# Five of 26 score masks of a cross attention are added by VectorE instead of TensorE

## The reference

```python
scores = jnp.einsum('bhqd,bhkd->bhqk', qh, kh) / jnp.sqrt(jnp.float32(D_K))
scores = jnp.where(mask == 0, NEG_INF, scores)
attn = jax.nn.softmax(scores, axis=-1)
ctx = jnp.einsum('bhqk,bhkd->bhqd', attn, vh)
```

## Time and profile before

| | us |
|---|---|
| median of 3 runs | 3214.25 (3211.05 to 3221.2) |
| profiled execution | 3217.97, its span 3216.2 |
| PE busy | 2959.7 (92%) |
| DVE busy | 2314.7 (72%) |
| ACT busy | 1707.0 (53%) |
| POOL busy | 455.9 (14%) |
| masked cross attention, first to last mask product | 696.1 to 1407.0 |

### The profile page before, as it was taken

One profiled execution on the slowest core, in us unless ns is written; L12 is line 12 of the kernel. 1 busy time (PEld: TensorE's weight loads), 2 busy tenths in 40 slices (PEclk: granted clock), 3 DMA queues, 4 the chain that ended last, 5 costly groups with the idle time before them and its releaser, 6 DMA issues. The chain is left out here.

```text
span 3216.2 us, 96994 instructions
## 1 busy us (share of the span) xinstructions
PE 2959.7 (92%) x41243; PEld 1694.4 (53%) x41243; DVE 2314.7 (72%) x5743; ACT 1707.0 (53%) x2152; POOL 455.9 (14%) x553
## 2 busy tenths in 40 slices
PE   5999999999999999982999999989999999989994
PEld 2666666546655565541466665553333333366662
DVE  6788888587777777748788886238999999551114
ACT  2366667525555555550477776312777777722220
POOL 0255562020000000000222212001100000001113
PEclk8899999979999999995899999997999999989997
DMA  2333432311000110110311111003121221121112
GB/s 71 114 116 107 115 98 73 107 47 24 23 15 24 24 25 17 26 24 18 108 39 39 40 44 45 25 32 98 27 51 50 67 58 31 34 86 42 46 40 75
DMA packets 129376, 172.62 MB, mean 54 GB/s; under 512 B 45199, under 2 KB 99087, under 8 KB 127343
## 3 DMA queue, kind: packets, MB, share of 16 engines
q1 hardware_dynamic: 112672, 119.09, 13.9%
q0 software_dynamic: 10800, 46.76, 4.5%
q10 hardware_dynamic: 5472, 0.56, 0.1%
HBM read 122.76 MB, written 35.16 MB: 49 GB/s over the span
## 5 line engine op out<-in xcount | busy, mean ns | idle before, releaser
L655 DVE TENSOR_REDUCE mpart<-ps 128x1 f32<-128x512 f32 (+5 forms) x2304 | 1247.2, 590 | 140.1 <-PE ps L488 79.1
L488 PE MATMUL ps<-stack 96*32 96x401 bf16 (+5 forms) x13312 | 1263.3, 355 | 21.9 <-DVE mpart L655 16.7
L512 PE MATMUL ps<-stack 99*32 99x512 bf16 (+3 forms) x11648 | 1135.2, 369 | 38.3 <-ACT xT L422 19.8
L422 ACT ACTIVATE xT<-ps 128x1024 f32<-128x1024 f32 (+3 forms) x800 | 732.4, 938 | 445.9 <-PE ps L512 235.2
L422 ACT ACTIVATE cn<-ps 128x1024 f32<-128x1024 f32 (+4 forms) x800 | 686.7, 870 | 321.6 <-PE ps L512 168.1
L488 PEld LDWEIGHTS ps<-stack 96*32 96x32 bf16 x13312 | 492.1, 96 | 516.5 <-DVE mpart L655 249.7
L651 DVE CUSTOM_DVE_ANT_0 scrap<-ps,arena 128x401 bf16<-128x401 f32 (+1 forms) x1024 | 550.7, 575 | 150.9 <-PE ps L488 127.0
L512 PEld LDWEIGHTS ps<-stack 99*32 99x32 bf16 x11648 | 415.4, 97 | 358.4 <-issue 122.0
L540 PE MATMUL ps<-xT,vall 128*17 128x512 f32 (+4 forms) x3648 | 455.1, 505 | 2.6 <-POOL xT L375 2.4
L540 PE MATMUL ps<-cn,vall 128*17 128x512 f32 (+3 forms) x3392 | 441.8, 497 | 0.9 <-ACT cn L422 0.9
L520 PE MATMUL ps<-arena,big 128*32 128x512 fp8e4 (+1 forms) x3264 | 360.4, 382 | 0.0
(11 more groups left out here) (246 smaller groups left out, 2561.4 us busy)
## 6 DMA issues: line engine op xcount, KB each, us to landing
stack<-q_parts SPq DMA_DIRECT2D x384, 64.0 KB, 2.6
wbuf<-in_mask POOLq DMA_DIRECT2D x16, 800.5 KB, 5.5
stack<-k_parts SPq DMA_DIRECT2D x192, 64.0 KB, 2.7
wbuf<-in_maskT POOLq DMA_DIRECT2D x12, 1024.0 KB, 5.4
arena<-in_moe_w SPq DMA_DIRECT2D x19, 512.0 KB, 4.5
stack<-k_parts SPq DMA_DIRECT2D x192, 50.0 KB, 2.2
stack<-sums_inverse SPq DMA_DIRECT2D x16, 512.0 KB, 5.6
parts<-osb SPq DMA_DIRECT2D x240, 32.0 KB
```

The lines of the kernel that those rows point to most:

```text
L422: nc.scalar.activation(e.prob[tile % P_SLOTS][0:rows, half * HALF + first:(half + 1) * HALF], S_PS(g)[0:rows, first:HALF], ACT.Exp, scale= ...
L488: last = nc.tensor.matmul(bank[quarter(j), 0:w], qs[b][0:KQ, t * P + 32 * j:t * P + 32 * j + 32], ks[b][0:KQ, a:a + w], start=True, stop=n ...
L512: last = nc.tensor.matmul(S_PS(g)[quarter(j), lo:hi], ks[b][0:KM, kt * P + 32 * j:kt * P + 32 * j + 32], qs[b][0:KM, half * HALF + lo:half ...
L655: nc.vector.tensor_reduce(dst, src, AX, ALU.max).then_inc(unit_used, 1)
```

## The change

In the masked attention the pieces n = 2, 7, 12, 17 and 22 of every head (`by_vector`) lose PE's mask product (8 matmuls each). DVE adds the mask in place in the two PSUM banks of the piece: `mask_scores`, one scalar_tensor_tensor of 128 x 1024 (mask times a constant plus scores), which waits for the scores (`s_ready`) and counts `s_masked`; ACT's exponential of such a piece waits for `s_masked`. The table `due` says before which unit DVE does it: before the first unit that PE issues in slot n-2, the slot in which PE also issues the scores of piece n. For the last pieces, when there are no units left, the masks stand behind `finish_max` and between `scale`, `invert` and `scale`. The other 21 pieces keep PE's product.

```diff
+    by_vector = [n for n in range(ns) if n % 5 == 2] if masked else []
+    due = {}
+    for h in range(H):
+        for n in by_vector:
+            turned = h + (1 if n - 2 <= turn else 2)
+            due[(turned, before[n - 2]) if turned < H else (H + h, n)] = (h, n)
...
-                        act.wait_ge(s_ready, g + 1)
+                        if n in by_vector:
+                            act.wait_ge(s_masked, h * len(by_vector) + by_vector.index(n) + 1)
+                        else:
+                            act.wait_ge(s_ready, g + 1)
...
+                    added_here = masked and n not in by_vector
...
-                                                    start=True, stop=not (crossed or masked))
+                                                    start=True, stop=not (crossed or added_here))
...
-                            if masked:
+                            if added_here:
...
+                def mask_scores(h, n):
+                    kt, rows, half = slots[n][0:3]
+                    dve.wait_ge(s_ready, h * ns + n + 1)
+                    to_mask = S_PS(h * ns + n)[0:rows]
+                    nc.vector.scalar_tensor_tensor(out=to_mask, in0=e.mask_one[0:rows, kt, half * HALF:(half + 1) * HALF],
+                                                   scalar=MASKED, in1=to_mask, op0=ALU.mult, op1=ALU.add).then_inc(s_masked, 1)
...
                     for u in range(nu):
+                        if (h, u) in due:
+                            mask_scores(*due[h, u])
                         if u < MAX_STEPS:
                             finish_max(h - 1, u)
                         unit(h, u)
...
                 for step in range(MAX_STEPS):
                     finish_max(H - 1, step)
+                for n in by_vector:
+                    if (2 * H - 2, n) in due:
+                        mask_scores(H - 2, n)
+                for n in by_vector[:2]:
+                    mask_scores(H - 1, n)
                 scale(0)
...
+                for n in by_vector[2:4]:
+                    mask_scores(H - 1, n)
                 invert(1)
+                for n in by_vector[4:]:
+                    mask_scores(H - 1, n)
                 scale(1)
```

More of the change, by code:

```diff
@@ L169, in attention_phase @@
         turned_back, fetched = sem("turned_back"), sem("fetched")
-        ahead_in, mask_in, mask_chain, selected = sem("ahead_in"), sem("mask_in"), sem("mask_chain"), sem("selected")
+        ahead_in, mask_in, mask_chain = sem("ahead_in"), sem("mask_in"), sem("mask_chain")
+        selected = sem("selected") if select else None
+        s_masked = sem("s_masked") if masked else None
         v_weights, v_source, v_bias = value
```

## The result

| | first kernel | changed kernel |
|---|---|---|
| median of 20 runs, us | 3214.32 (3205.68 to 3232.98) | 3230.17 (3218.85 to 3244.33) |
| profiled execution, us | 3217.97 | 3233.98 |

The changed kernel is slower: ratio 1.0051, 95% interval 1.0034 to 1.0068, or 16.4 us (11 to 22) of 3214. The forecast was 20.5 us more, 3235; the measured time lies inside its range, 3203 to 3262.

What follows compares the result with a forecast made beforehand. PE, busy 614.91 of 616 us in the masked cross attention, was taken as the bound. Its saving of 34.9 us against new waits worth some 55 us made 20.5 us more: 3235 us for the median, range 3203 to 3262.

Steps and rivals of the forecast that it cites:

- PE sets the pace, and its saving counts: Masked cross attention: PE is busy 614.91 of 616 us, so every microsecond taken from it counts unless its waits grow.
- The gross figure of 34.9 (3179): Mask products removed from PE: 2.18 us per head, 34.9 us over 16 heads; 3179 us if nothing else happened.
- The operation: DVE's added mask operation, 80 in all: 1.28 us from start to end, 1.18 until the next can start.
- The chain around a piece: Waits of PE for banks and of ACT for the mask around masked pieces: 1.23 us more a head.
- the maximum's transfer: Head ends: piece 22's mask puts finish_max about 1.3 us later; next head's scores(0) move by the same order, costing nothing.
- The end of the stage: Last five masked pieces, without units beside them: +0.45 us each, 2.25 us in all.
- The cover for scale(1): Stage end: invert(1) and scale(1) end near 1410, before the last head's first inverse needs DVE, so no cost.
- A (saving in part): Rival: PE's saving comes through in part; 3207 us with half the waits gone, 3179 with all gone; chance 0.15.
- B (about even): Rival: within 0.3%; mask at 1.07 us a piece and waits a tenth shorter, +9.5, 3224 us; chance 0.22.
- C: Rival: the mask operation on DVE is dearer, 1.50 us, 21 us more: 3256 us; chance 0.15.
- D: Rival: PE's clock falls in the new gaps; a tenth of the stage at 1.2 GHz, 3271 us; chance 0.03.

## Why the prediction was right

**PE sets the pace, and its saving counts.** Right: 26 us (stage) to 30 us (ratio) less without DVE's work. The gross figure of 34.9 (3179) was a bound and 5 to 9 us too good. Most of this is piece 2, where the removed steps gave nothing (4.05 and 4.06; 0.44 in each of 15 heads is 6.6 us); the rest is lost at 7, 17 and 22.

**The operation.** 1.28 us from start to end and 1.18 from start to start were taken; it measured 1.224 and 1.13. The row with 0.75 us at 512 columns (L632) misled: the new operation has exactly the time of the two-input rows, 0.692 at 512 and 1.224 at 1024, against 0.69 and 1.22 there. This term was mis-sized by 0.05 us an operation; with 60 to 65 us a microsecond that is some 3 of the 4.1 us between forecast and result (5.3 by the stage). The Trainium skill ("VectorE: DVE Perf Modes", the errata section) gives (columns + 151) cycles at 0.96 GHz for a two-input fp32 addition, an estimate of 1.224 us for 1024 columns; this run shows 1.224 with the scores in PSUM. Its 120 + columns for a PSUM source, which I weighed, gives an estimate of 1.19, and the run doesn't bear that out.

**The chain around a piece.** The steps held in order and size: mask start 0.72 (0.75 measured), the unit that waits at 2.53 (996.60 - 994.09 = 2.51), piece 7 by its backlog at 1.37 (the mask at 986.03, scores at 984.66) and then by the exponential. For pieces 7, 12, 17, 22 and 2 the sums were 0.48, 0.26, 0.06, 0.43 and 0; measured 0.41, 0.23, 0.02, 0.32 and -0.08, together 0.91 a head in place of 1.23. The largest miss is piece 22, whose own terms (0.26 + 0.15) make 0.41 and not 0.43. That piece 2 got shorter was not forecast, and no run shows why. Moving PE's units behind the product and moving the mask by one unit showed each of the two chains as the cause. The agreement piece by piece is what bears the prediction out: the range of 59 us, from a gain of 11 to a loss of 48, would have held much else.

**Taken too lightly: the maximum's transfer.** I wrote that the waits in slots 20 and 21 would keep scores(0) in step with it. In the changed kernel that was nearly so (0.04 us a head at piece 24, waits of 1.7 us in all); the run with the units behind the product showed that it held only because PE was late: as soon as PE was faster there, 7.1 us of wait came.

**The end of the stage.** 2.25 us forecast for the pieces without units; the last two heads' spans grew by 1.11 and 1.65 (from 43.65 and 34.86 us), of which 0.58 belongs to the pieces 2, 7, 12 and 17 of head 14, so 2.2: right. The cover for scale(1) held, but with less to spare: invert(1) moved behind the mask of piece 17, and scale(1) ran beside the very end:

```profile
1421.27 2.36 DVE L708 TENSOR_TENSOR parts<-parts,stack 128x1024 f32<-128x1024 f32 x2 [1.91 <-DMA stack<-sums_inverse]
...
1427.43 0.96 DVE L715 RECIPROCAL osb<-ps 128x128 f32<-128x128 f32 x1 [3.80 <-PE ps L614]
```

3.8 us of idle time are left before the first inverse; in the first kernel there were 17:

```profile
1412.37 0.96 DVE L695 RECIPROCAL osb<-ps 128x128 f32<-128x128 f32 x1 [17.00 <-PE ps L601]
```

**The rivals.** A (saving in part) did not come; what it needed, an operation whose occupancy (start to start) is under 0.86 us, is what the run with half of the columns had with 0.60, and its 18 us gained lie between A's two figures, 7 and 35. B (about even) did not come either, but was not far: it needed 1.07, and 1.13 was measured; its +9.5 lies just outside the 11 to 22 measured. Its sum is also off: 65 x 0.11 and a tenth of the 55 us of waits make 12.7 and not 11, so +7.8. C and D did not come: the operation was shorter than taken, and the clock stayed at 1.00.

## What to carry to other kernels

Before work is moved from a full engine to one with idle time, write down what stands behind it in the second engine's order and who waits for that: here DVE was idle for 22% of the stage, and an operation of 1.2 us still cost more than it saved, because PE's next units needed banks that DVE would free behind it, or ACT's exponential came too late for PE's next scores. Then look for work of the full engine that depends on neither, and put it into the gap; here that was the product with the values, and with four even pieces the order of PE's units around it made the difference of 1% between a loss and a gain. Choose the pieces by where the second engine stands when they come, and keep away from the stretch that feeds a transfer.

## What the runs showed of the hardware

A DVE operation with the input and the output in PSUM (fp8 mask from SBUF, fp32 scores in place) took 1.224 us for 1024 columns and 0.692 for 512, the same as a two-input operation wholly in SBUF (1.222): the fp8 input and PSUM at both ends added nothing that shows beside that row. The next DVE operation, on another bank, started 1.13 us after it (994.84 to 995.97), 0.09 before its recorded end; behind the operation of 512 columns it was 0.60.
